# A decoder's routing norms, logits and top choices, moved from the mixture-of-experts stage into the BiDAF stage, with 16-bit one-hots

## The reference

```python
def _L1_xattn_ref(c, q, w_cq, b_cq, w_c, b_c, w_q, b_q, W_l, b_l):      # BiDAF; q is 16 x 120 x 256
    cq = jnp.einsum('bcd,bqd,d->bcq', c, q, w_cq) + b_cq
    s = (c @ w_c + b_c)[:, :, None] + (q @ w_q + b_q)[:, None, :] + cq
    a = jax.nn.softmax(s, axis=2)
    c2q_att = jnp.einsum('bcq,bqd->bcd', a, q)
    b_att = jax.nn.softmax(jnp.max(s, axis=2), axis=1)
    q2c_att = jnp.einsum('bc,bcd->bd', b_att, c)[:, None, :]
    x = jnp.concatenate([c, c2q_att, c * c2q_att, c * q2c_att], axis=-1)
    return x @ W_l.T + b_l

def _L1_ffn_ref(input_emb, W1, b1, W2, b2, Wr, br):                     # 8 experts, the best 2 a token
    logits = jnp.einsum('bsd,de->bse', input_emb, Wr) + br
    route_w = jax.nn.softmax(logits, axis=-1)
    _, topk_idx = jax.lax.top_k(route_w, TOP_K)
    mask = jax.nn.one_hot(topk_idx, E, dtype=route_w.dtype).sum(-2)
    routed = route_w * mask
    routed = routed / routed.sum(axis=-1, keepdims=True)
    h = jax.nn.relu(jnp.einsum('bsd,edh->ebsh', input_emb, W1) + b1[:, None, None, :])
    expert_out = jnp.einsum('ebsh,ehd->ebsd', h, W2) + b2[:, None, None, :]
    return jnp.einsum('bse,ebsd->bsd', routed, expert_out)
```

## Time and profile before

| | us |
|---|---|
| median of 3 runs | 3789.82 (3786.21 to 3791.73) |
| the profiled execution | 3788.22 |
| its span | 3786.4 |
| busy in the span: TensorE, VectorE, GpSimd, ScalarE | 3288.4, 2719.1, 2068.0, 1203.2 |
| BiDAF, from its first norm to its last moments | 2948.0 to 3153.4 |
| head of the mixture of experts, to the table | 3154.5 to 3251.5 |
| its loop | 3251.5 to the end |

### The profile page before, as it was taken

How to read it: one execution, slowest core, us unless ns; L and a number is a source line. 1 busy time by engine, 2 the same in 40 slices (tenths; PEclk the granted TensorE clock), 3 DMA queues, 4 the chain that set the end, 5 groups by cost and what they waited for, 6 DMA issues and landing times. The chain is left out here.

```text
span 3786.4 us, 93267 instructions
## 1 busy us (share of the span) xinstructions
PE 3288.4 (87%) x33694; PEld 2790.3 (74%) x33695; DVE 2719.1 (72%) x10688; ACT 1203.2 (32%) x3140; POOL 2068.0 (55%) x2392
## 2 busy tenths in 40 slices
PE   6999957786599999999999999978888897699998
PEld 4777735554488888888888888855564687699998
DVE  6666634554999999999999999948887554533333
ACT  1443435552222222222222222225664221122221
POOL 4444335551677777777777777858885000233333
PEclk8999978997799999999999999989999896799999
DMA  5444434443000000000000000034453115466665
GB/s 152 110 108 110 109 83 116 123 113 122 1 2 2 2 2 2 2 2 2 2 2 2 2 2 2 2 91 124 125 130 74 34 33 160 123 181 183 182 182 136
DMA packets 256114, 277.90 MB, mean 73 GB/s; under 512 B 44001, under 2 KB 200673, under 8 KB 255201
## 3 DMA queue, kind: packets, MB, share of 16 engines
q1 hardware_dynamic: 242081, 253.69, 23.5%
q0 software_dynamic: 13632, 18.91, 3.3%
HBM read 187.63 MB, written 72.29 MB: 69 GB/s over the span
## 5 line engine op out<-in xcount | busy, mean ns | idle before, releaser
L1190 POOL TENSOR_TENSOR peer_hot_v<-peer_hot_e,peer_parts 80x512 bf16<-80x512 bf16 x768 | 990.9, 1316 | 320.9 <-DVE peer_hot_e L1233 311.7
L1009 PE MATMUL peer_ps_u<-peer_up,peer_g 128*128 128x256 f32 x2048 | 534.3, 408 | 0.6 <-DVE x_all L1331 0.6
L990 PEld LDWEIGHTS peer_ps_h<-peer_xnT,peer_down 128*128 128x128 f32 x4096 | 512.7, 197 | 15.7 <-DMA peer_down<-in_peer_down 0.9
L990 PE MATMUL peer_ps_h<-peer_xnT,peer_down 128*128 128x128 f32 x4096 | 512.3, 280 | 0.6 <-DMA peer_down<-in_peer_down 0.6
L1000 PE MATMUL peer_ps_w<-peer_hot_v,peer_hot_u 80*128 80x32 bf16 x12288 | 347.3, 177 | 145.4 <-DVE peer_g L1245 97.5
L1000 PEld LDWEIGHTS peer_ps_w<-peer_hot_v,peer_hot_u 80*128 80x128 bf16 x12288 | 337.0, 97 | 167.3 <-issue 92.1
L1009 PEld LDWEIGHTS peer_ps_u<-peer_up,peer_g 128*128 128x128 f32 x2048 | 393.1, 202 | 53.5 <-issue 1.0
L1087 ACT ACTIVATE peer_g<-peer_ps_h 128x512 f32<-128x512 f32 x256 | 152.9, 597 | 840.5 <-PE peer_ps_h L990 840.2
L1237 DVE TENSOR_TENSOR peer_hot_u<-peer_count,peer_uvT 80x2048 bf16<-80x2048 bf16 x256 | 349.4, 1365 | 0.0
L2072 POOL DMA_INDIRECT out<-moe_y,moe_target x71 | 112.6, 1585 | 312.6 <-DVE moe_y L2203 309.6
L2007 PE MATMUL moe_ps_t<-moe_xgT,moe_w 128*128 128x128 f32 x2272 | 267.3, 276 | 0.0
(11 more groups left out here) (362 smaller groups left out, 7073.9 us busy)
## 6 DMA issues: line engine op xcount, KB each, us to landing
moe_w<-in_moe_w SPq DMA_DIRECT2D x142, 512.0 KB
causal_qs<-causal_qscratch SPq DMA_DIRECT2D x32, 384.0 KB, 3.9
cross_qs<-cross_qscratch SPq DMA_DIRECT2D x32, 384.0 KB, 3.6
band_qs<-band_qscratch SPq DMA_DIRECT2D x32, 384.0 KB, 4.1
moe_w<-in_moe_w SPq DMA_DIRECT2D x8, 1024.0 KB, 11.7
causal_qscratch<-causal_part SPq DMA_DIRECT2D x32, 192.0 KB, 2.6
causal_kscratch<-causal_part SPq DMA_DIRECT2D x32, 192.0 KB, 2.0
causal_ks<-causal_kscratch SPq DMA_DIRECT2D x32, 192.0 KB, 4.2
```

The source lines that it names most:

```text
L990: mm = nc.tensor.matmul(ps_h[:, n % 2, k * P:(k + 1) * P], down[:, c, 4 * n + k, :], xnT[:, par, c, :], start=(c == 0), stop=(c == DC - 1))
L1009: mm = nc.tensor.matmul(ps_u[:], g[:, par, v, :], up[:, v, :], start=(v == 0), stop=(v == EV - 1))
L1190: ins = nc.gpsimd.tensor_tensor(hot_v[0:SEL, n % RING, part], hot_e[0:SEL, n % RING], w, ALU.mult)
```

## The change

It makes the head's first part inside BiDAF, and shortens the making of the table.

- A new `Route` holds what both stages use (weights, constants, `xn`, `logit`, `top`, `topi`, a DRAM tensor of rows). It is opened ahead of BiDAF and closed, as a `Room` of its own, after the last stage.
- BiDAF's `halves` runs to `B + 5`. For batch `h - 2` VectorE makes the reciprocal roots without ScalarE: `bn_aggr`, an integer first guess and three Newton rounds (`guess_root`, `newton(1)` to `newton(3)`), all on 128 x 2. For batch `h - 3` GpSimd norms the rows (`norm_rows`), SyncE stores them, TensorE transposes them into the row's bank `p1` (`turn_x`), ScalarE copies them out (`take_x`), and TensorE makes the logits in `p2`. For batch `h - 4` VectorE adds the bias and picks.
- BiDAF's own `norm` moves from VectorE to GpSimd. VectorE's order is new.
- SyncE loads the constants in half 1 and one expert's `w2` in each of halves 2 to 9.
- `moe_stage` begins with the exponentials' differences. The one-hots are 16-bit, with token pairs innermost, made for 8 tiles at a time in 4 rounds without reuse of buffers: `tilehot` and `tilename` (128 x 1136 each), `rowhot` (128 x 2048). A token has one name of 16 bits instead of two of 8. The list of experts is made in the first round, and SyncE starts on `w1` with it.

```diff
-def bidaf_stage(nc, stats, ident, d):
+def bidaf_stage(nc, stats, ident, d, route):
...
-            for h in range(B + 2):
+            for h in range(B + 5):
...
+            def store_rows(z, n, b):
+                sp.wait_ge(z.xn_ready, n + 1)
+                tiles = slice(b * TT, (b + 1) * TT)
+                sp.dma_start(xn_rows[:, tiles, 0:D], route.xn[:, z.k]).then_inc(route.rows_out[z.k], 16)
...
+            for h in range(B + 4):
                 if h < B:
                     fetch(streams[h % NS], h // NS, h)
-                if 0 <= h - 2 < B - NS:
+                if h == 1:
+                    weights()
+                if 0 <= h - 2 < B:
                     store(streams[h % NS], (h - 2) // NS, h - 2)
+                if 0 <= h - 3 < B:
+                    store_rows(streams[(h - 3) % NS], (h - 3) // NS, h - 3)
+                if 2 <= h < 2 + E:
+                    sp.dma_start(route.w2[:, h - 2], w2_in[:, h - 2]).then_inc(route.weights, 16)
...
             def row(z, n, b):
                 pe.wait_ge(z.t_used, n + 1)
                 wait(pe, z.wad_ready, n)
+                wait(pe, z.l_used, n - 1)
...
+            def turn_x(z, n, b):
+                pe.wait_ge(z.xn_ready, n + 1)
+                pe.wait_ge(z.acol_ready, min(n + 2, B // NS))
+                for t in range(TT):
+                    for c in range(DC):
+                        at = (t * DC + c) * P
+                        mm = nc.tensor.transpose(z.p1[:, at:at + P], route.xn[:, z.k, t, c * P:(c + 1) * P], ident[:])
+                mm.then_inc(z.xt_done, 1)
+
+            def logits(z, n, b):
+                pe.wait_ge(z.xt_used, n + 1)
+                pe.wait_ge(z.wad_ready, min(n + 2, B // NS))
+                pe.wait_ge(route.loaded, 16 * route.NLOAD)
+                for t in range(TT):
+                    for c in range(DC):
+                        mm = nc.tensor.matmul(z.p2[:, t * E:(t + 1) * E], route.xnT[:, t, c, :], route.wr[:, c, :],
+                                              start=(c == 0), stop=(c == DC - 1))
+                mm.then_inc(z.l_done, 1)
+
             halves([(turn_prob, 1), (col, 1), (turn, 0), (attend, 1), (q2c, 1), (row, 0), (project_a, 1), (scores, 0),
-                    (project_ca, 1), (top, 0), (project_c, 1)])
+                    (project_ca, 1), (turn_x, 3), (top, 0), (project_c, 1), (logits, 3)])
...
-            halves([(take_prob, 1), (take, 0), (take_a, 1), (exps, 0), (eexp, 0)])
+            halves([(take_prob, 1), (take, 0), (take_a, 1), (exps, 0), (eexp, 0), (take_x, 3)])
+
+        @block.gpsimd
+        def _(pool):
+            def norm(z, n, b):
+                if b == 0:
+                    pool.wait_ge(ready, 1)
+                wait(pool, z.q2c_done, n)
+                for t in range(TT):
+                    ins = nc.gpsimd.tensor_scalar(z.c[:, t, :], x_all[:, b * TT + t, :], mean[:, b * TT + t, :],
+                                                  rstd[:, b * TT + t, :], ALU.subtract, ALU.mult)
+                ins.then_inc(z.c_ready, 1)
+
+            def norm_rows(z, n, b):
+                pool.wait_ge(z.roots_ready, n + 1)
+                wait(pool, z.xt_done, n)
+                wait(pool, route.rows_out[z.k], 16 * n)
+                for t in range(TT):
+                    ins = nc.gpsimd.tensor_scalar(route.xn[:, z.k, t, :], x_all[:, b * TT + t, :], stats.mv[:, b * TT + t, 0:1],
+                                                  route.guess[:, z.k, t:t + 1], ALU.subtract, ALU.mult)
+                ins.then_inc(z.xn_ready, 1)
+
+            norm(streams[0], 0, 0)
+            halves([(norm, -1), (norm_rows, 3)])
...
+            def guess_root(z, n, b):
...
+                for t in range(TT):
+                    ins = nc.vector.bn_aggr(stats.mv[:, b * TT + t, :], stats.moments[:, b * TT + t, :])
+                links.link(ins)
+                links.link(nc.vector.tensor_scalar(var, stats.mv[:, tiles, 1], EPS, None, ALU.add))
+                links.link(nc.vector.tensor_scalar(i, var.bitcast(I32), 1, None, ALU.logical_shift_right))
+                nc.vector.tensor_scalar(g.bitcast(I32), i, -1.0, float(0x5f3759df), ALU.mult, ALU.add).then_inc(z.guess_ready, 1)
+                links.again()
+
+            def newton(k):
+                def roots(z, n, b):
...
+                    dve.wait_ge(z.guess_ready, 3 * n + k)
+                    links.link(nc.vector.tensor_tensor(q, g, g, ALU.mult))
+                    links.link(nc.vector.tensor_tensor(q, q, var, ALU.mult))
+                    links.link(nc.vector.tensor_scalar(q, q, -0.5, 1.5, ALU.mult, ALU.add))
+                    nc.vector.tensor_tensor(g, g, q, ALU.mult).then_inc(z.guess_ready if k < 3 else z.roots_ready, 1)
+                    links.again()
+                return roots
...
-            norm(streams[0], 0, 0)
-            halves([(take_col, 1), (make_m, 0), (add, 2), (make_row, 0), (make_wad, 1), (product, 1), (norm, -1), (rowmax, 0),
-                    (moments, 2), (normalise, 0), (find_top, 0), (batch_row, 0)])
+            halves([(take_col, 1), (add, 2), (make_m, 0), (take_logit, 4), (moments, 2), (make_row, 0), (make_wad, 1), (product, 1),
+                    (guess_root, 2), (newton(1), 2), (newton(2), 2), (rowmax, 0), (newton(3), 2), (normalise, 0), (find_top, 0),
+                    (batch_row, 0), (pick, 4), (constants, 3)])
...
             for n in range(NHOT):
...
+                few = slice(n * FEW, (n + 1) * FEW)
+                one_hot(tilehot, tileb, JT, few)
+                nc.vector.tensor_tensor(rowhot[:, few], iota2[:].unsqueeze(1).broadcast_to((P, FEW, P, TOPE)),
+                                        rowb[:, few, :].unsqueeze(2).broadcast_to((P, FEW, P, TOPE)), ALU.is_equal)
+                nc.vector.tensor_tensor(tilename[:, few], tilehot[:, few],
+                                        name[:, few, :].unsqueeze(2).broadcast_to((P, FEW, JT, TOPE)), ALU.mult).then_inc(hot_ready, 1)
```

More of the change, by code:

```diff
@@ L1391, with __init__ @@
 TOKENS = B * S
-def bidaf_stage(nc, stats, ident, d):
+E = 8
+TOPE = 2
+HID = 4 * D
+HC = HID // P
+HB = HC // 2
+ROW = D + E
+JT = (TOKENS * TOPE + E * (P - 1)) // P
+MAXT = TOKENS // P
+class Route:
+    def __init__(self, nc, ctx):
+        self.nc = nc
+        r = Room(nc, ctx, "route")
+        sb, sem = r.sb, r.sem
+        self.w2 = sb("w2", [P, E, HC, D])
+        self.b1 = sb("b1", [P, E, HC])
+        self.b2 = sb("b2", [P, E, D])
+        self.wr = sb("wr", [P, DC, E])
+        self.br = sb("br", [P, E])
+        self.iota = sb("iota", [P, P])
+        self.pid = sb("pid", [P, 1])
+        self.tri32 = sb("tri32", [P, P])
+        self.tri = sb("tri", [P, 2, P], BF16)
+        self.iota2 = sb("iota2", [P, P, TOPE], F16)
+        self.spare = sb("spare", [P, 1])
+        self.steps128 = sb("steps128", [P, MAXT])
+        self.namef = sb("namef", [P, TILES])
+        self.name = sb("name", [P, TILES, TOPE], F16)
+        self.below = sb("below", [P, E, E])
+        self.xn = sb("xn", [P, NS, TT, D])
+        self.xnT = sb("xnT", [P, TT, DC, P])
+        self.var = sb("var", [P, NS, TT])
+        self.guess = sb("guess", [P, 2, TT])
+        self.half = sb("half", [P, 2, TT], I32)
+        self.sq = sb("sq", [P, 2, TT])
+        self.logit = sb("logit", [P, TILES, E])
+        self.top = sb("top", [P, TILES, 8])
+        self.topi = sb("topi", [P, TILES, 8], U32)
+        self.rows = nc.dram_tensor("moe_xn_rows", (TOKENS, ROW), F32).ap()
+        self.loaded = sem("loaded")
+        self.weights = sem("weights")
+        self.const_ready = sem("const_ready")
+        self.x_out = sem("x_out")
+        self.rows_out = [sem(f"rows_out{k}") for k in range(NS)]
+        self.gates_out = sem("gates_out")
+    NLOAD = 7
+def bidaf_stage(nc, stats, ident, d, route):
     x_all, mean, rstd = stats.x_all, stats.mean, stats.rstd
@@ new lines, in take_logit, with pick @@
+            def take_logit(z, n, b):
+                tiles = slice(b * TT, (b + 1) * TT)
+                dve.wait_ge(z.l_done, n + 1)
+                nc.vector.tensor_tensor(route.logit[:, tiles, :], z.p2[:, 0:TT * E].rearrange("p (t e) -> p t e", e=E),
+                                        route.br[:].unsqueeze(1).broadcast_to((P, TT, E)), ALU.add).then_inc(z.l_used, 1)
+            def pick(z, n, b):
+                dve.wait_ge(z.l_used, n + 1)
+                for t in range(b * TT, (b + 1) * TT):
+                    ins = nc.vector.max(route.top[:, t, :], route.logit[:, t, :])
+                steps.link(ins)
+                for t in range(b * TT, (b + 1) * TT):
+                    nc.vector.max_index(route.topi[:, t, :], route.top[:, t, :], route.logit[:, t, :])
@@ new lines, in _ @@
+            dve.wait_ge(expert_ready, 1)
+            dve.wait_ge(hot_used, 1)
+            placed = ps_y[:, 0, 0:JT]
+            nc.vector.tensor_scalar(empty[:], placed, 0.0, route.spare[:], ALU.is_equal, ALU.mult)
```

(4 more changed lines are left out.)

276 lines of the change are left out of this document (94 added, 182 removed).

## The result

The changed kernel takes 3762.66 us (median of 4 runs, 3756.01 to 3767.81) against 3788.80 (4 runs) before: ratio 0.993, 95% interval 0.9912 to 0.9947. It is 26 us faster. The forecast was 3805, slower by 16. Its profiled execution lasted 3762.07 us, 3760.3 of it the span, against 3788.22 and 3786.4 before: 26.1 us of span to explain.

A forecast was written before the change was run, and what follows sets the result against it. It took TensorE to bound BiDAF before, and a VectorE and ScalarE chain after. 3788.2 - 71.4 (head) + 77.1 (BiDAF) + 10 (clock) + 1.0 (barrier) = 3804.9 us, range 3762 to 3825.

The forecast's parts named there:

- Two signs: Listed for the changed profile: BiDAF period near 13.6 with VectorE's durations unchanged; gap at `turn` caused by the `q` DMA.
- the two take turns: BiDAF: whichever of VectorE and GpSimd comes second waits for the other's current instruction to end; GpSimd's take 1.216 us.
- The walk: One BiDAF half followed in time through GpSimd's norms, `product`, roots, `rowmax` and logits: 16.70 us, 4.81 more.
- 16.7 rather than 15.4: BiDAF half length: 16.7 us if `make_wad`'s two-input instruction also alternates with GpSimd, 15.4 if it does not.
- hardly disturb one another: Rival for BiDAF: engines do not alternate, half 13.61 us, BiDAF pays 34, clock holds, total 3752; chance 0.17.
- TensorE gets about 0.96 a half: BiDAF: four added transposes (0.42 us) and four logit matmuls, half of the eight in 0.95.
- "Covered", of `q`: BiDAF: the next `q` DMA goes out near 10.7 us and is wanted at 17.8, so its delay costs nothing.
- The fourth rival: BiDAF: `q` behind 1 MB loads up to 4 us late in eight halves, or clock always low; 3820 to 3850, chance 0.14.
- The clock, +10: BiDAF: narrow TensorE work brings half-clock spells in about every second half, six to seven at 1.7 us; between 0 and 22.
- The tail and the head: Behind BiDAF: half 16 loses 2.6 us, the last batch's uncovered chain 9.1; the head saves 71.4, 56.1 of it before `topf`.
- Table: Head: new one-hots and table take 14.9 us instead of 30.2, saving 15.3.
- An earlier `w1` gives nothing: Experts' start: loading `w1` sooner saves no time, as the first tile waits for gathered rows.

The follow-up runs named there:

- fetch_first: Changed kernel with SyncE asking for the next `q` ahead of `store_rows` and the 1 MB load; 3741.20 us, ratio to before 0.9879.
- the meter: Separate kernel timing VectorE instructions alone and beside GpSimd's; eight products took 4.91 us alone, 5.30 beside one-input, 12.54 beside two-input instructions.
- logits_twice: On fetch_first, TensorE makes each batch's logits twice; 3782.01 us, one run.
- old_table: On fetch_first, the one-hots, table and experts' list are those of the kernel before; 3764.02 us, ratio to before 0.9928.
- late_expert: On fetch_first, the experts' list is made in the last round of one-hots instead of the first; 3745.09 us, ratio to before 0.9881.

## Why the prediction was wrong

Two signs that the forecast had named for being wrong came true: a period near 13.6 with VectorE's durations close to those of before (13.17 measured), and a gap at `turn` with the `q` DMA as its cause.

**What failed is one step: "the two take turns".** The walk let each of GpSimd's four instructions hold VectorE for its whole 1.216 us, and 3.1 of the 4.81 us a half came from that (the same walk without turns gives 13.61). It had `product` end at 9.6. Measured: `product` ends at 6.1, VectorE's instructions beside GpSimd lose about 0.55 us a half (0.2 of it `product`, 0.17 the end of `newton(1)`), and the half grows by 1.28. Halves 2 to 15 were to cost 64.4 us; without the late `q` they cost about 17 (16.6 by the steady halves, 17.0 in fetch_first). That difference of 47 is more than the whole miss of 43. The step came from the earlier trace rows: a 16-bit VectorE instruction of 2.06 us, and GpSimd's `tensor_scalar` of 2.18 beside it. I read the pair as two engines that hold each other. But a GpSimd `tensor_tensor`, a two-input instruction, ran until 981.36, into the first 0.97 us of the VectorE one; by the meter that is what lengthened it, and the 2.18 us show GpSimd giving way, which is what its one-input form does. The short row of that group (0.42 us at 0.87) also stood beside the two-input form. GpSimd at these two moments of the kernel before:

```profile
976.98 4.38 POOL L1190 TENSOR_TENSOR peer_hot_v<-peer_hot_e,peer_parts 80x512 bf16<-80x512 bf16 x3
...
1507.38 7.20 POOL L1190 TENSOR_TENSOR peer_hot_v<-peer_hot_e,peer_parts 80x512 bf16<-80x512 bf16 x6
```

None of the rows showed VectorE held by a `tensor_scalar`. The third row, a VectorE `tensor_scalar` of 4.60 us that ended with a memset, stays open: a memset has no tensor input, and no run here measured one beside VectorE.

The Trainium skill's "SBUF — State Buffer", section "SBUF: two separate sides", on which I leaned for 16.7 rather than 15.4, has a VectorE instruction with two SBUF inputs and any GpSimd instruction that reads SBUF exclude one another. The meter disagrees: GpSimd's one-input instructions read SBUF too, and they cost eight products 0.4 us in all. Only beside its two-input form did the engines alternate, and there VectorE's forms with one tensor input did as well.

**The rival "hardly disturb one another"** (3752, given 0.17) had the mechanism between the engines. Its half of 13.61 was measured at 13.17, and its 34 us for the BiDAF would be 29.2 without the late `q` (16.6 for the halves, 1.2 at the start, 11.4 at the end, which is 56.1 - 44.7). The late `q`, which it did not have, puts 19.2 back. What it had wrong is what sets the half: TensorE's own work, not VectorE's chain.

**"TensorE gets about 0.96 a half"**: mis-sized. The row of eight in 0.95 us is four matmuls in the code, each recorded twice, so the logits take 0.89 (logits_twice) and the transposes, by subtraction, the remaining 0.39: 1.28. With TensorE the bound, this term decided the half.

**"Covered", of `q`**: wrong in this kernel, and wrong because of the other error. The forecast had it issued at 10.7 and wanted at 17.8 of a 16.7 us half. It went out 9.9 us into the half and landed 5.5 later; `turn` wanted it at 14.1, 0.9 into the next half. Had the half been as long as forecast, the same transfer would have been in time. The fourth rival named the mechanism (behind the 1 MB loads), and gave it 0.14 and the wrong sign of the total.

**The clock, +10**: about 13.6 in the trace, but by another route, so that the two numbers lie close is luck. I expected spells from narrow work alone, in every second half. With `q` in time there were none in 13 halves with all that work. Here they came behind the waits. logits_twice, with more narrow work, had seven without a wait, so the mechanism exists; it did not act here.

**The tail and the head** held, each as a sum; their parts were not measured one by one. Half 16 and the uncovered chain less the head's 56.1: -44.4 forecast, -44.7 measured. Table: -15.3 forecast, -15.7 measured, and old_table gives it back. First norm on GpSimd +1.0: +1.2. "An earlier `w1` gives nothing": it gave 2.7, since gathered rows and `w1` no longer leave at the same time (late_expert, where the rows landed 2.5 us later); I had looked at who waits for `w1`, not at what leaves just ahead of the gather. The second `Room`'s barrier cost no more than the 0.3 us by which everything behind the first expert matmul grew.

In sum, from the last `turn_prob` to the table it was -60.4 against -59.7 forecast, -2.7 came on top behind the table, and 36.7 instead of 75.4 up to the last `turn_prob`.

## What to carry to other kernels

Before letting two engines take turns in a walk, ask which of the two gave way in each row, and what the other ran just before; a pair of stretched instructions does not say who held whom. A load that nothing waits for still delays what is issued just behind it: issue it after the small transfer that the bound engine needs next. Moving it to another engine's queue is not shown to help; an experiment that changes the queue and the order at once does not tell which of them acted. A gap of a microsecond on TensorE can cost several, because the clock can fall behind it. And cover worked out from one wrong duration is wrong with it.
